# The second inverse of a pair ahead of the wait for the stored means on GpSimd, and the shifts ahead of the first context evacuation on VectorE

## The reference, cut to what matters

```python
xn = _layernorm(x, gamma_media, beta_media)        # context (8, 722, 512)
ln = _layernorm(latents, gamma_lat, beta_lat)      # latents (8, 100, 512)
q = ln @ Wq + bq
kv = jnp.concatenate([xn, ln], axis=1) @ Wkv + bkv
sim = jnp.einsum('bhid,bhjd->bhij', q * DH ** -0.5, k)   # 8 heads
out = jnp.einsum('bhij,bhjd->bhid', jax.nn.softmax(sim, axis=-1), v)
return out.transpose(0, 2, 1, 3).reshape(b, -1, INNER) @ Wo + bo
```

## Time and profile before

| | |
|---|---|
| time, median of 3 runs | 1073.04 us (1069.95 to 1073.32) |
| profiled execution: time / span | 1065.5 us / 1063.8 us |
| granted TensorE clock, mean | 0.977 of full speed |
| TensorE matmuls busy | 1006.2 us, 95% |
| VectorE / ScalarE / GpSimd busy | 819.4 / 586.0 / 179.7 us |

### The profile page before, as it was taken

The page is one execution under the profiler, slowest core; times in us unless marked ns, Lnnn a source line. Parts: engine busy times, 40 slices in busy tenths (PEclk is TensorE's granted clock), DMA queues, the critical chain, the costliest instruction groups (busy, mean ns, idle before and its releaser), DMA issues.

```text
span 1063.8 us, 14901 instructions
## 1 busy us (share of the span) xinstructions
PE 1006.2 (95%) x5274; PEld 923.1 (87%) x5275; DVE 819.4 (77%) x1083; ACT 586.0 (55%) x766; POOL 179.7 (17%) x169
## 2 busy tenths in 40 slices
PE   8999999799989989899899999999998999999995
PEld 7969999798979979899798899997977888888884
DVE  7888457897978969889697877886768956947981
ACT  4527565555536445464364654674635856837871
POOL 3624000120121111201203000000012111211320
PEclk9999999989999999999899999999998999999998
DMA  9333987461732916529066121869367974947960
GB/s 280 112 127 131 310 273 220 142 132 40 189 74 71 214 40 170 92 55 208 31 179 115 32 86 28 289 230 346 114 178 245 361 259 161 360 161 249 371 231 10
DMA packets 107117, 183.88 MB, mean 173 GB/s; under 512 B 27936, under 2 KB 48928, under 8 KB 107058
## 3 DMA queue, kind: packets, MB, share of 16 engines
q1 hardware_dynamic: 102834, 172.64, 52.7%
q0 software_dynamic: 4224, 10.46, 4.0%
HBM read 146.94 MB, written 37.11 MB: 173 GB/s over the span
## 4 chain that ended last, share of the span: by engine, by line
PE 70%; issue 10%; DVE 9%; DMA 5%; POOL 3%; SPq 1%; ACT 1%; DVEq 0%; POOLq 0%; ACTq 0%
PE bank L585 19%; PE bank L586 19%; PE bank L587 19%; DMA sm<-scr_inverse 2%; DVE str__65 L1728 2%; PE bank L1165 2%; PE bank L1346 2%; DMA w<-in_WoT 1%; PE bank L1070 1%; PE bank L1072 1%; PE bank L1071 1%; POOL rsr L856 1%; DMA zr<-scr_z 1%; PE bank L1196 1%; POOL rsr L858 1%
## 5 line engine op out<-in xcount | busy, mean ns | idle before, releaser
L1744 DVE TENSOR_TENSOR wsl<-stage,wsh 128x2048 fp32r<-128x2048 f32 x63 | 143.7, 2292 | 21.8 <-ACT wsh L1534 17.1
L585 PE MATMUL bank<-ph,xn_h 128*128 128x400 f32 x384 | 143.0, 372 | 0.0
L586 PE MATMUL bank<-pl,xn_h 128*128 128x400 f32 x384 | 134.6, 351 | 0.0
L585 PE MATMUL bank<-qt_h,xt_h 128*128 128x400 f32 x384 | 134.4, 350 | 0.0
L587 PE MATMUL bank<-ph,xn_l 128*128 128x400 f32 x384 | 133.8, 349 | 0.0
L586 PE MATMUL bank<-qt_l,xt_h 128*128 128x400 f32 x384 | 132.5, 345 | 0.0
L587 PE MATMUL bank<-qt_h,xt_l 128*128 128x400 f32 x384 | 132.1, 344 | 0.0
L1534 ACT CAST wsh<-stage 128x2048 fp32r<-128x2048 f32 x63 | 120.5, 1920 | 10.8 <-PE bank L587 9.1
L1507 ACT ACTIVATE zf<-zf,gbm 128x400 f32<-128x400 f32 x64 | 39.8, 627 | 132.5 <-DVE zf L2010 132.5
L1484 ACT ACTIVATE pa<-bank,rsr 128x400 f32<-128x400 f32 x96 | 56.7, 593 | 81.8 <-PE bank L587 81.7
L586 PEld LDWEIGHTS bank<-pl,xn_h 128*128 128x128 f32 x384 | 74.6, 194 | 3.2 <-issue 1.6
(11 more groups left out here) (278 smaller groups left out, 2408.0 us busy)
## 6 DMA issues: line engine op xcount, KB each, us to landing
stage<-in_W SPq DMA_DIRECT2D x63, 1024.0 KB, 6.4
scr_q<-st SPq DMA_DIRECT2D x16, 800.0 KB, 6.5
qf<-scr_q SPq DMA_DIRECT2D x16, 800.0 KB, 7.0
scr_z<-zf SPq DMA_DIRECT2D x16, 800.0 KB, 4.4
zr<-scr_z SPq DMA_DIRECT2D x16, 800.0 KB, 6.3
rt<-in_ctxT SPq DMA_DIRECT2D x7, 1444.0 KB, 20.8
raw<-in_ctx SPq DMA_DIRECT2D x8, 768.0 KB, 5.7
raw<-in_ctx SPq DMA_DIRECT2D x8, 512.0 KB
```

What stands on the lines that cost most here:

```text
L585: pe.matmul(dest, lh, rh, start=start and k == 0, stop=False)
L586: pe.matmul(dest, lh, rl, start=False, stop=False)
L1744: return dve.tensor_tensor(dst, src, high.bitcast(F32), ALU.subtract)
```

## The change

On GpSimd, inside the loop over b, the order inverse 2b, store means b+2, load means b+2, deviations b+2, inverse 2b+1 becomes inverse 2b, store means b+2, inverse 2b+1, load means b+2, deviations b+2. The mean transfers count on a semaphore of their own with the mean loads (s_mrow) and no longer on that of the inverses (s_kept). Ahead of the loop, rows_std(1) now stands ahead of load_mean(1). On VectorE, shifts(u) stands ahead of weighted(u-1, 0) in every turn from 2 to 14; in turn 1 too this is so of the pair shifts(1), weighted(0, 0).

```diff
             def store_mean(b):
...
                     pool.dma_start(d_row[b].rearrange("(c p) -> p c", p=P)[:, cs], mvs[b % 2][:, cs, 0],
-                                   allow_slow_non_contiguous=True).then_inc(s_kept, 16)
+                                   allow_slow_non_contiguous=True).then_inc(s_mrow, 16)
             def load_mean(b):
-                pool.wait_ge(s_kept, kept("mean", b))
+                pool.wait_ge(s_mrow, 48 * b - 16)
                 pool.wait_ge(s_nr, (b - 1) * 2)
                 pool.dma_start(mrow[:], bc(d_row[b, 0:MEDIA], MEDIA)).then_inc(s_mrow, 16)
...
-                pool.wait_ge(s_kept, kept("inverse", u))
+                pool.wait_ge(s_kept, 32 * u + 16)
                 pool.dma_start(sm[:, 1, :], bc(d_iv[u], GR)).then_inc(s_kept, 16)
-                pool.wait_ge(s_kept, kept("rows", u))
+                pool.wait_ge(s_kept, 32 * u + 32)
...
             store_mean(1)
+            rows_std(1)
             load_mean(1)
-            rows_std(1)
             for b in range(B - 1):
                 spread_inverse(2 * b)
                 if b + 2 < B:
                     store_mean(b + 2)
+                spread_inverse(2 * b + 1)
+                if b + 2 < B:
                     load_mean(b + 2)
                     rows_std(b + 2)
-                spread_inverse(2 * b + 1)
...
-                    dve.wait_ge(s_mrow, 16 * b)
+                    dve.wait_ge(s_mrow, 48 * b)
...
                 if g:
                     for k in range(3):
                         keys_transposed(b + 1, k)
+                    shifts(u)
                     weighted(u - 1, 0)
-                    shifts(u)
                     keys_transposed(b + 1, 3)
                 else:
                     if b + 1 < B:
                         queries(b + 1, 0)
+                    shifts(u)
                     weighted(u - 1, 0)
-                    shifts(u)
```

More of the change, by code:

```diff
@@ L913, in router_std @@
                 pool.sem_inc(s_rsx, 1)
[L915 to L923, removed]
             def store_mean(b):
```

## The result

| | before | after |
|---|---|---|
| time, median (range) | 1073.1 us (1069.95 to 1073.32) | 1033.8 us (1031.78 to 1042.73) |
| ratio, 95% interval | | 0.966 (0.960 to 0.971) |
| profiled execution: time / span | 1065.5 / 1063.8 us | 1042.7 / 1041.0 us |
| the same kernel profiled again: time / span | | 1032.8 / 1031.0 us |
| granted TensorE clock, mean | 0.977 | 0.985; again 0.986 |

The forecast was 1039.5 us, 1033 to 1050, a ratio of 0.969. The median lies in that range, 0.8 us above its lower end. The medians lie 39 us apart and the ratio makes it 37, where 33.5 were forecast.

The account below looks back on a forecast made before the run. TensorE, busy 95%, was taken as the bound, losing time in stalls at L1165 and slow tails. Gains of 29.7 + 2.2 + 2.1 less 0.5 made 33.5 us: 1065.5 to 1032.0, scaled to 1039.3, stated as 1039.5, range 1033 to 1050.

Parts of the forecast that it names:

- The bound and the cause: TensorE, busy 95%, waits 30.6 us at L1165 for `dg`; VectorE waits for `inv`, GpSimd for the stored means.
- Turns 4 to 12, 29.7 us: Ten intervals between L1165s fall from 342.2 to 312.5 us as five stalls and five slow tails go.
- the sum: Whole-kernel gain: 29.7 + 2.2 + 2.1, less 0.5 for small waits at the edges, 33.5 us.
- `dg` early by 0.15 us: Turn 6: VectorE's shifts behind the queries end at 377.7, before TensorE is ready for L1165 at 377.87; no stall.
- the 0.5 that I had named as the sign: Sign of being right: L1165 waits under 0.5 us in turns 2 to 12.
- rival B: VectorE is held up beside GpSimd, `dg` 0.5 us late in turn 6; about 2 us in all, 1041 to 1044; 14%.
- `inv` 8.9 us behind `iv`: Turn 6, inverse's way through GpSimd: store 3.1 and load 3.5 us between bounds, `inv` at 375.5 after reciprocals at 366.6.
- the row of the rule (11.0): Turn 6: if completions land after older writes, the inverse's store is done at 372.6 with the queries, `inv` at 377.6.
- Rival A: The inverse stays late: the wait moves to context(5, 2), 2.3 us in six turns, up to 14 us; 1045 to 1053; 17%.
- Turn 2 and turn 1, 2.2 and 2.1: Turn 2 loses its stall of 2.24 us; turn 1 gains 2.1 us from earlier shifts, its inverse's DMA waits remaining.
- Costed at nothing: Odd turns' evacuation 1.7 us later, the later mean load hidden by 3.7 us, and rows_std(1) moved ahead: no cost.
- the scaling: Profile to median: the shown median, 0.7% above the profiled execution, keeps that ratio, making 1032.0 into 1039.3 us.

Follow-up runs that it names:

- e2: GpSimd's new order and semaphores with VectorE's old order, evacuation ahead of the shifts, against the changed kernel; 1047.32 us, ratio 0.974.
- e3: VectorE's new order alone, with GpSimd's old one, against the kernel before; 1049.27 us, ratio 0.978.
- e1: The changed kernel run and profiled again, nothing edited; 1035.28 us, ratio 0.965.
- e9: The changed kernel once more, unedited, as control of a later group of runs; 1033.78 us, ratio 0.964.
- e8: The changed kernel with load_mean(1) back ahead of rows_std(1) before the loop; 1031.19 us, one run.
- e4: The changed kernel with VectorE's shifts of even turns ahead of the queries too; 1038.58 us, ratio 0.968.
- e5: The changed kernel with SyncE loading the next queries only when the second inverse's store is done; 1046.19 us, one run.
- e10: The changed kernel with SyncE loading a batch's second queries ahead of the context rows in odd turns; 1033.04 us, ratio 0.965.

## Why the prediction was right, point by point

- **The bound and the cause.** Right. The wait at L1165 was that of the inverse behind the means, handed on by VectorE's order. One reading was off: VectorE's seventh wait for `inv` is turn 15's; in turn 2 it waited for `inv` too, but the profile puts those 3.73 us down to TensorE. e2 and e3 each take away one link, and each leaves a part of it: the short wait for `dg` and the longer one for `zf`.
- **Turns 4 to 12, 29.7 us.** Right in kind: the stalls and the five tails went together. The size, 342.20 to 312.46 in e1, is right to 0.1 us only in the best of three profiles. In the first and in e9 the late second queries gave 9.3 and 5.1 us of it back, a cost that the sum doesn't have:

```profile
274.44:596.23 321.79, 313.52 (x1742) 308.11 (x1742) 286.87 (x407) 175.51 (x250) 43.44 (x55) 0.99 0.53 120
```

- **`dg` early by 0.15 us.** Right in kind: no wait over 0.42 us in turns 2 to 12 of e1; in the first profile 0.75 in turn 6 and 0.73 in turn 12, above the 0.5 that I had named as the sign. The waits that are left have rival B in them: a shift instruction of 0.16 us took 0.53 beside the copy in turn 6 of the first profile, and 0.81 in turn 12 of e1:

```profile
367.62 0.53 DVE L1943 TENSOR_TENSOR rmc<-rm,c 100x4 f32<-100x4 f32 x1
...
553.08 0.90 POOL L935 COPY inv<-sm 128x400 f32<-128x400 f32 x1 [3.58 <-DMA sm<-scr_inverse]
553.19 0.81 DVE L1943 TENSOR_TENSOR rmc<-rm,c 100x4 f32<-100x4 f32 x1
...
554.90 0.94 PE L1156 MATMUL bank<-dg,ones 100*128 100x400 f32 x2 [0.42 <-DVE dg L1947]
```

- **`inv` 8.9 us behind `iv`.** The size was off. It was 10.45 (355.79 to 366.24) in e1. The mis-sized term is the store's wait, 5.24 for my 3.1; the load's was 2.86 for my 3.5. I took the store from a value between the two rows and gave it room, although the queries' load was in flight: the row of the rule (11.0) was nearer. It cost nothing, since VectorE came to the evacuation at 366.99, 0.7 later. Rival A was that close: e3 shows its form, and its price when it holds, 2.6 us a turn.
- **Turn 2 and turn 1, 2.2 and 2.1.** Right as a sum. Turn 1's wait of 6.33 us became 3.62 to 4.25 (I had said 3.8), and turn 2's 2.24 went. From L1156 of turn 0 to that of turn 2 the three profiles of the changed kernel took 58.2, 57.0 and 58.9 us against 62.7: 3.8 to 5.7 us less, for my 4.3. How it divides between the turns a single profile doesn't fix, since the interval from turn 1 to turn 2 alone ranged from 31.1 to 35.5 over the profiles of these kernels.
- **Costed at nothing.** Right: `mrow` was not waited for, the later evacuation in odd turns left the interval 4 to 5 at 31.03, and rows_std(1) did nothing (e8).
- **Rival B.** It is there, though small where it counts. In the changed kernel VectorE's shifts are held up beside the copy in most even turns (by up to 0.7 us), but TensorE pays 0.42 us of waits for it in e1 and at most 1.9 in the first profile, near the 2 us of the rival. e4 has it on GpSimd's side in five turns, at up to 1.7 us for a copy.
- **From the profile to the median.** Here lie the other 4 to 6 us, and the step of the forecast that was off. The two profiled spans differ by 32.8, near the sum's 33.5, in part by luck: the turns gained 35.6, and 2.8 were lost where nothing had been changed. The timed runs differ by 37 to 39. The profiled execution of before was better than any other run of it: in later comparisons 33 runs of before took 1066.2 to 1078.1 us, the lower third at a mean clock of 0.974, the upper third at 0.970. I had scaled the sum up by 0.7% in proportion, to 1039.3. The changed kernel's medians (1033.8 to 1035.3) lie 0.1 to 0.2% over its second profile's 1032.8, and near what the sum gave without the scaling (1032.0); only the kernel before ran 0.7% over its profile. So the scaling was wrong, and the range held by a margin of 0.8 us. That more of before's turns have tails in its usual runs fits the lower clock (0.004 of 1070 us is 4.3 us of work at full clock, and the two thirds lie 7.4 us apart), but no trace of such a run is here, so it stays open which turns.

## What to carry to other kernels

When a wait is handed on through three engines, price each link with the others in their new places: here either reordering alone gave about two thirds of the gain of both, since they remove the same wait. A small DMA that is a handshake took here as long as the bulk load that was issued just ahead of it, though on another queue; place it ahead, or give it the load's time, and look whether the load then becomes the late one (e5). And before a median is carried over from a profile, ask where in the spread of runs this profile lies, and which late transfer makes that spread.

## What the runs showed of the hardware

- Executions of the identical kernel differed by 7 to 8 us at one place through one transfer: the second queries of batch 5 landed 23.7 and 21.7 us behind their issue in two profiles; in a third no load of queries took more than 18.8. Where they are issued ahead of the context rows (e10) none took more than 16.7.
- A stall's length alone doesn't decide whether a tail at half clock follows: 2.24 us had none and 2.81 had one (before, turns 2 and 8: intervals of 31.19 and 32.71 us), 2.93 had one (e2), 3.48 had none (e3, at another place of the turn).
- GpSimd's copy of 0.89 us took 1.94 to 2.57 beside a VectorE instruction of 1.82 us (e4) and ended 0.74 to 0.76 us behind it each time; VectorE's instruction of 0.16 us took 0.34 to 0.89 beside the copy (three profiles of the changed kernel) and ended within 0.03 us of it.
- A store of 1.6 KB waited 1.42 us with no bulk load issued just ahead of it (e5), and 4.40 to 5.97 behind a load of 800 KB that another engine had issued 1.3 us earlier (the changed kernel, turn 6 of three profiles).
